# Third dense pair of a graph network kernel: half of its node batches moved beside two convolutions, raw rows looked up again

## The reference, cut to what matters

```python
x = layernorm(x + gat3(x))        # L0: three attention layers over 4 heads, with raw x as the residual
x = layernorm(x + gcn2(x))        # L1: two convolutions, relu(agg @ W1.T + b1), relu(agg @ W2.T + b2)
x = layernorm(x + gcn1(x))        # L2: one convolution
x = layernorm(x + sage2(x))       # L3: relu(concat(h, mean of neighbours) @ W + b), twice
```

## Time and profile before

| | |
|---|---|
| median of 3 runs | 5128.42 us (5124.89 to 5132.35) |
| the profiled execution | 5132.61 us, its span 5130.8 us |
| busy share of the span | PE 77%, DVE 76%, ACT 67%, POOL 55% |
| instructions | 108022 |
| DMA | 1072.25 MB, mean 209 GB/s |
| HBM | read 607.70 MB, written 466.24 MB |

### The profile page before, as it was taken

The page is one execution under the profiler, slowest core; times in us unless marked ns, Lnnn a source line. Parts: engine busy times, 40 slices in busy tenths (PEclk is TensorE's granted clock), DMA queues, the critical chain, the costliest instruction groups (busy, mean ns, idle before and its releaser), DMA issues. The chain is left out here.

```text
span 5130.8 us, 108022 instructions
## 1 busy us (share of the span) xinstructions
PE 3927.6 (77%) x23872; PEld 2892.8 (56%) x23872; DVE 3884.4 (76%) x14954; ACT 3424.7 (67%) x11259; POOL 2796.4 (55%) x2718
## 2 busy tenths in 40 slices
PE   2999999566996898774998995897767676665554
PEld 1666766344774454663555774343666666565554
DVE  4999999676998787997886998898547777444343
ACT  0899999454886676884776885787548788333332
POOL 2888888475552122651223452112767676777777
PEclk9999999787998899997999997998888888997666
DMA  2566665597996576994676995675546565543332
GB/s 62 165 187 196 202 194 190 194 331 274 355 353 220 196 242 209 328 326 152 228 241 234 349 350 189 221 225 170 157 152 202 187 208 189 156 146 113 96 97 72
DMA packets 612938, 1072.25 MB, mean 209 GB/s; under 512 B 107736, under 2 KB 128362, under 8 KB 612764
## 3 DMA queue, kind: packets, MB, share of 16 engines
q1 hardware_dynamic: 537308, 944.74, 54.2%
q0 software_dynamic: 75456, 125.65, 9.2%
HBM read 607.70 MB, written 466.24 MB: 209 GB/s over the span
## 5 line engine op out<-in xcount | busy, mean ns | idle before, releaser
L2409 POOL DMA_INDIRECT got_c<-table,src_row x980 | 931.3, 950 | 378.8 <-issue 296.5
L1410 POOL DMA_INDIRECT src_got_s<-table,src_row x588 | 554.4, 943 | 497.4 <-PE bank L1456 119.4
L1994 POOL TENSOR_TENSOR part_m<-part_m,half_sum_m 128x512 f32<-128x512 f32 x147 | 220.7, 1501 | 916.8 <-DVE half_sum_m L2210 916.8
L2437 PE MATMUL bank<-pick_c,got_c 128*128 128x128 f32 x1960 | 348.3, 333 | 407.9 <-DMA got_c<-table,src_row 337.2
L2003 PE MATMUL bank<-w_all,dt_m 128*128 128x512 f32 x1176 | 568.7, 600 | 35.4 <-DMA dt_m<-delta_t 33.6
L2437 PEld LDWEIGHTS bank<-pick_c,got_c 128*128 128x128 f32 x1960 | 299.9, 234 | 453.6 <-issue 251.6
L1565 ACT ACTIVATE z_s<-z_s,shift_s,dev_s 128x128 f32<-128x128 f32 x1176 | 483.4, 485 | 2.1 <-DVE shift_s L1684 0.9
L2540 ACT COPY agg_c<-bank 128x512 f32<-128x512 f32 x245 | 143.0, 584 | 434.7 <-DVE bank L1851 281.4
L790 PEld LDWEIGHTS bank<-w_mean,ht 128*128 128x128 f32 x2352 | 313.5, 194 | 144.0 <-issue 144.0
L2461 PE MATMUL bank<-w_c,agg_c 128*128 128x128 f32 x1960 | 389.3, 328 | 2.3 <-ACT agg_c L2540 2.2
L787 PE MATMUL bank<-bias,first_row 128*128 128x512 f32 x588 | 323.6, 632 | 38.1 <-ACT ht L850 13.8
(11 more groups left out here) (327 smaller groups left out, 11582.0 us busy)
## 6 DMA issues: line engine op xcount, KB each, us to landing
table<-rows SPq DMA_DIRECT2D x294, 256.0 KB
x_s<-table SPq DMA_DIRECT2D x294, 256.0 KB
x_c<-table SPq DMA_DIRECT2D x245, 256.0 KB
table<-mid_s SPq DMA_DIRECT2D x196, 256.0 KB
table<-z_s SPq DMA_DIRECT2D x196, 256.0 KB
table<-z_c SPq DMA_DIRECT2D x196, 256.0 KB
own_rows_s<-table SPq DMA_DIRECT2D x147, 256.0 KB
pick_t_s<-picks_t SPq DMA_DIRECT2D x147, 256.0 KB
```

Of the source, the lines that this page charges most:

```text
L1410: nc.gpsimd.indirect_dma_start(out=src_got[r][:, g, :], out_offset=None, in_=tables[l].rows, in_offset=bass.IndirectOffsetOnAxis(ap=src_ro ...
L2409: nc.gpsimd.indirect_dma_start(out=got[r][:, g, :], out_offset=None, in_=t_in.rows, in_offset=bass.IndirectOffsetOnAxis(ap=src_row[:, t:t ...
L2437: ins = nc.tensor.matmul(b_sum[r][:, k * P:(k + 1) * P], got[b.slot][:, k, :], pick[r][:, k, :], start=k == 0, stop=sage, skip_group_check ...
```

## The change

Four things:
1. `edge_scores(2)` is called with `solo=True`. It then handles only the even node batches (0, 2, ..., 96), one in each of its 49 steps instead of two, with a step order of its own (`step_solo`) on PE, ACT, DVE and SP, and other waits that pace POOL's gathers. Buffers and banks alternate by the step's parity.
2. `convolve` takes a further argument `nodes`. With it, every second step also does one node batch of the third pair: convolution 0 does the odd batches 1 to 49, convolution 3 the batches 49, 51, ..., 97 (25 each, batch 49 in both). The node work's bias copy, PSUM to SBUF copies and normalisation are ACT's, the residual and the statistics DVE's.
3. `edge_scores(1)`: `set_by_dve` is now `(0,)`, so that PE writes the bias of h = 1, and DVE's `set_bias(b, 1)` goes.
4. The table `raw_slots` goes, with its store in `first_slots`, POOL's wait for that store and the load in `attend(2)`. There POOL gathers the raw rows again from `x`: two gathers before the addition of the batch and two after it, in a fully unrolled loop.

```diff
@@ first_slots, sync
-                            b = at(1)
-                            if b:
-                                sp.wait_ge(gathered[b.slot], b.ring4(64))
-                                sp.sem_inc(sp_pace, 1)
-                                sp.dma_start(batch_rows(raw.slots, b.batch()),
-                                             x[b.slot][:, :, :].rearrange("p g d -> p (g d)")).then_inc(raw_out[b.slot], 16)
@@ first_slots, gpsimd
-                                pool.wait_ge(raw_out[r], 16 * (b // 4))
@@ edge_scores
-                set_by_dve = (0, 1)
+                set_by_dve = (0, 1) if first else (0,)
...
@@ edge_scores, sync
+                        def step_solo(at):
+                            b = at(0)
+                            if b:
+                                loads(b)
+                            b = at(5)
+                            if b:
+                                store_middle(b, 0)
+                                store_delta(b)
+                                store_score(b)
+                            b = at(6)
+                            if b:
+                                store_rows(b, 0)
@@ edge_scores, gpsimd pace
+                            elif solo:
+                                if g == 1:
+                                    pool.wait_ge(h_made, b - 2)
+                                elif g == 2:
+                                    pool.wait_ge(y_made, b - 3)
+                                else:
+                                    pool.wait_ge(turned, b - 1)
@@ edge_scores, tensor
+                        def step_solo(at):
+                            b = at(1)
+                            if b:
+                                hidden(b, 0)
+                            b = at(2)
+                            if b:
+                                turn_delta(b)
+                                product(b, 0)
+                                turn_hidden(b, 0)
+                            b = at(3)
+                            if b:
+                                score(b)
+                            b = at(0)
+                            if b:
+                                turn_rows(b, 0)
+                            b = at(1)
+                            if b:
+                                spread(b)
@@ edge_scores, scalar: step_solo is relu(b-1), deviation(b-3), delta_out(b-2), normalise(b-3), turn_out(b), score_out(b-3)
@@ edge_scores, vector
-                            b = at(0)
-                            if b:
-                                set_bias(b, 1)
...
+                        def step_solo(at):
+                            b = at(3)
+                            if b:
+                                scale(b, 0)
+                            b = at(2)
+                            if b:
+                                residual(b, 0)
+                                middle(b, 0)
+                                moments(b, 0)
+                            b = at(1)
+                            if b:
+                                set_bias(b, 0)
+                                difference(b)
@@ attend, gpsimd
+                        if last:
+                            for b in range(nb):
+                                r = b % 2
+                                if b > 3:
+                                    pool.wait_ge(z_read, b - 3)
+                                raw_rows(b, (0, 1))
+                                pool.wait_ge(m_made, 4 * b + 4)
+                                nc.gpsimd.tensor_tensor(flat(part[r]), flat(part[r]), flat(half_sum[r]), ALU.add).then_inc(parts_added, 1)
+                                raw_rows(b, (2, 3))
@@ convolve
+                def even(b):
+                    return nodes and b and b.slot % 2 == 0
@@ convolve, sync
+                        def load_nodes(b):
+                            r = b.slot // 2
+                            hold(sp, nz_read, b.ring(1, -2))
+                            sp.sem_inc(sp_pace, 1)
+                            sp.dma_start(flat(nx[r]), batch_rows(from_rows.nodes, b.batch() + offset)).then_inc(nx_in[r], 16)
...
+                            b = at(3)
+                            if even(b):
+                                load_nodes(b)
...
+                            b = at(6)
+                            if even(b):
+                                store_node_middle(b)
+                            b = at(9)
+                            if even(b):
+                                store_nodes(b)
@@ convolve, tensor
+                        def node_turn(b):
+                            r = b.slot // 2
+                            pe.wait_ge(nx_in[r], b.ring4(16))
+                            hold(pe, nmid_made, b.ring(1, -1))
+                            for g in range(GB):
+                                ins = nc.tensor.transpose(b_turn[:, g * P:(g + 1) * P], nx[r][:, g, :], ident[:, :])
+                            ins.then_inc(n_turned, 1)
...
+                        def node_steps(at):
+                            b = at(4)
+                            if even(b):
+                                node_middle(b)
+                            b = at(5)
+                            if even(b):
+                                node_product(b)
+                            b = at(3)
+                            if even(b):
+                                node_hidden(b)
...
                         def step_gcn_relu(at):
                             b = at(1)
                             if b:
                                 sum_edges(b)
+                            node_steps(at)
                             b = at(2)
                             if b:
                                 product(b)
+                            if even(b):
+                                node_turn(b)
                             b = at(1)
                             if b:
                                 add_own(b)
@@ convolve, scalar
+                        def node_middle_out(b):
+                            r = b.slot // 2
+                            act.wait_ge(nmid_turned, b.ring(1))
+                            hold(act, nmid_stored[r], b.ring4(16, -16))
+                            nc.scalar.copy(flat(nmid[r]), b_turn[:, :]).then_inc(nmid_made, 1)
+                            hold(act, nz_read, b.ring(1, -1))
+                            nc.scalar.copy(b_node[:, :], nb2[:, :]).then_inc(n_bias, 1)
...
+                        def node_steps(at):
+                            b = at(3)
+                            if even(b):
+                                node_relu(b)
+                            b = at(4)
+                            if even(b):
+                                node_middle_out(b)
+                            b = at(6)
+                            if even(b):
+                                node_deviation(b)
+                            b = at(7)
+                            if even(b):
+                                node_normalise(b)
+
                         def step_relu(at):
                             b = at(0)
                             if b and not sage:
                                 diagonals(b)
+                            node_steps(at)
                             b = at(2 if sage else 1)
                             if b:
                                 set_bias(b)
                                 sums_out(b)
+                            b = at(2)
+                            if even(b):
+                                node_turned(b)
@@ convolve, vector, step_relu
+                            b = at(6)
+                            if even(b):
+                                node_scale(b)
                             b = at(2)
                             if b:
                                 residual(b)
+                            b = at(5)
+                            if even(b):
+                                node_residual(b)
+                                node_moments(b)
@@ the calls
-        edge_scores(2, (io["L3_gnn_W1"][0:D, :], io["c_L3_gnn_b1"]), (io["L3_gnn_W2"][0:D, :], io["b_L3_gnn_b2"]), t[6], t[7], t[8])
+        edge_scores(2, (io["L3_gnn_W1"][0:D, :], io["c_L3_gnn_b1"]), (io["L3_gnn_W2"][0:D, :], io["b_L3_gnn_b2"]), t[6], t[7], t[8], True)
...
+        third = (t[6], t[7], t[8], (io["L3_gnn_W1"][0:D, :], io["c_L3_gnn_b1"]), (io["L3_gnn_W2"][0:D, :], io["b_L3_gnn_b2"]))
+        convolve(0, "gcn0", False, t[3], t[4], None, (io["L1_gnn_W1"],), io["b_L1_gnn_b1"], third + (1,))
...
+        convolve(3, "sage", False, t[6], t[7], None, (io["L3_gnn_W1"][D:, :], io["L3_gnn_W1"][0:D, :]), io["b_L3_gnn_b1"],
+                 third + (2 * (nb - (nb + 1) // 2) + 1,))
```

More of the change, by code:

```diff
@@ L1243, in edge_scores @@
                 scores = pairs("scores", (P, P))
-                x, z = ([fours(f"{n}{h}_") for h in range(2)] for n in ("x", "z"))
+                halves = range(1 if solo else 2)
```

(31 more changed lines are left out.)

222 lines of the change are left out of this document (156 added, 66 removed).

## The result

The changed kernel takes 5277.92 us (median of 4 runs), the kernel before 5130.39 beside it: ratio 1.0285, 95% interval 1.0258 to 1.0312. The profiled execution's span is 5280.9 us, 150.1 more than before. The forecast was 5325, slower.

The account below looks back on a forecast made before the run. No engine is full; stages in a row have different limits, POOL's gather issue bounding the convolutions. Terms -67 + 25 + 253 - 9 - 8 + 2 = +196 us on 5128.4 gave 5325 us, range 5215 to 5445.

Parts of the forecast that it names:

- Fourth convolution: ACT and PE take turns because node steps precede the sums; 20.1 us a pair, 512 us against 259, +253.
- 17.7 at full clock: Fourth convolution: a pair of steps from PE's 9.94, ACT's 7.33 and four hand-overs of 0.1 us, PE unthrottled.
- Rival 1: Fourth convolution: ACT's node work is hidden, costing 25 us; whole kernel 5096 us, faster; 7%.
- rival 2: Fourth convolution: PE falls to its lower clock level for most of it, 628 us; whole kernel 5441 us; 13%.
- Third score stage: Solo halves the dense batches; a loop through PE and DVE then bounds the step at 6.1 us, 326 against 393, -67.
- First convolution: Node work makes PE and ACT as long as POOL's period; 10.7 us a pair plus 8 us at the end, +25.
- late nx load: First convolution: upper bound of +68 us, 12.5 us a pair, if the nx load lands after PE wants it.
- Second score stage: Bias moves from DVE, the fullest engine, to PE, the new limit at about 6.15 us a step, -9.
- slots: Slots stage: 49 stores of 256 KB and POOL's wait for them go, -8, bounds 0 and -17.
- Last message pass: Raw load leaves SP and 196 gathers come to POOL, covered by 0.67 us a step if they stay 0.95 us, +2.
- rival 4: Last message pass: POOL's addition comes late, DVE's two-input operations lengthening gathers, +34; whole kernel 5357 us; 4%.
- the 0.17 that the slack held: Last message pass: POOL's addition is late if the gathers grow by over 0.17 us each; slack 0.67 us a step.

Follow-up runs that it names:

- h: Changed kernel plus two thrown-away 512-wide products on PE in each fourth-convolution step with node work: 5207.96 us, ratio 1.0150 to the kernel before.
- a_sums_first: Changed kernel with ACT's set_bias and sums_out ahead of its node steps in the fourth convolution; on slow gathers 5627.97 us, ratio 0.9984 to the kernel before.
- b: Changed kernel with only ACT's square root and normalising operations moved behind sums_out in the fourth convolution: 5723.40 us, ratio 1.0152 to the kernel before, slow gathers.

## Why the prediction was right, point by point

**Fourth convolution (+253, measured +256).** The mechanism and the size held. The step that carried it was to read both engines' new orders for the same n and to ask which item of ACT's step PE's product waits for. That the number came out within 3 us is in part luck, since two terms missed and cancel. A pair was put at 20.1 us and took 20.0 on average, 20.45 in the steady part. ACT's items with four hand-overs were put at 7.7 us, and PE's pauses for them are 6.6 (2.87 + 3.78 in the pair shown): the items were added by their durations, but each starts before the record of the one ahead ends (copy to copy 0.48 us, 0.59 long), and a hand-over takes 0.04 to 0.06 us, not 0.1. PE's own part was put at 12.4 and took 13.4 (13.8 in the pair shown), which is 1.35 to 1.39 times the 9.94 and not 1.25 (start and drain took 34 us, not 30): the assumed clock was a choice between ends of 1 and 1.73, and its reason, the first convolution's 0.85, was thin. The working's 17.7 at full clock carries the same excess: with 6.6 it is 16.5, and h, at 0.92, has 16.9. Rival 1 (hidden hand-over) and rival 2 (628 us) did not come. Rival 1's condition had a slip: with 21 us of start and drain 57 us more allow a pair of 12.3 us, not 11.5; at 20 neither matters. The low end of the range had one too: 57 us less in the fourth convolution and 33 less by solo lead from 5325 to 5235, not 5215.

**Third score stage (-67, measured -96): the mis-sized term.** The loop was named rightly, its length was not: 6.1 us against 5.5. I added durations. What counts is from start to start, and that is shorter, as the changed kernel's trace shows: on DVE 0.60 us from the residual to the copy, 0.69 and 0.68 long, and on PE 0.50 from the transposes to the product, where the transposes are 0.66 long:

```profile
2900.52 0.69 DVE L1716 SCALAR_TENSOR_TENSOR z_s<-bank,x_s 128x512 f32<-128x512 f32 x1 [1.04 <-PE bank L1471]
...
2901.12 0.68 DVE L1710 COPY mid_s<-bank 128x512 f32<-128x512 f32 x1
...
2904.34 0.66 PE L1492 MATMUL bank<-ident,delta_s 128*128 128x128 f32 x4 [0.78 <-DVE delta_s L1703]
...
2904.84 1.06 PE L1471 MATMUL bank<-w_s,ht_s 128*128 128x128 f32 x8
```

**First convolution (+25, measured +14).** Two steps stayed at POOL's 10.0 us; the gathers run from 3463.1 to 3707.2 as tightly as before. The 0.7 us a pair that I added for two engines that are as long as POOL was not there. The drain behind the last gather was larger than the 8 us: 3735.8 - 3708.2 = 28 us, where it was 13. The late nx load that I bounded at +68 is real and small, and POOL's lead of four batches hides it (waits view, first convolution):

```profile
POOL got_c L2531 <- issue: 58.5, 192, 0.3
...
PE bank L2599 <- DMA nx_c<-table: 23.5, 20, 2.8
```

**Second score stage (-9, measured -15)** and **slots (-8, measured -4)**: within their bounds, right in sign; for the first the reason (DVE full, PE next) is not shown, since on slow gathers undoing it gained.

**Last message pass (+2, measured -2).** Right in size by luck: the reason given, gathers of 0.95 us, was wrong. (The -2 itself is no gain: other quick traces of the same stage are up to 1.6 us longer.) I wrote that no row of gathers shows the contention of the Trainium skill's page (GPSIMD Engine Reference, Specifications). The groups view and the timeline of the changed kernel do:

```profile
L2052 POOL DMA_INDIRECT x_m<-in_x_dram,dst_node x196 | 222.5, 1135 | 100.7 <-issue 52.0 <-POOLq L117 48.4
L2062 POOL TENSOR_TENSOR part_m<-part_m,half_sum_m 128x512 f32<-128x512 f32 x49 | 62.5, 1275 | 7.2 <-DVE half_sum_m L2280 6.4
```

```profile
3300.98 1.31 POOL L2052 DMA_INDIRECT x_m<-in_x_dram,dst_node  x1 [0.30 <-issue]
3302.60 1.36 POOL L2052 DMA_INDIRECT x_m<-in_x_dram,dst_node  x1 [0.30 <-issue]
...
3305.42 0.96 POOL L2052 DMA_INDIRECT x_m<-in_x_dram,dst_node  x1 [0.16 <-issue]
```

```profile
3300.80 0.68 DVE L2304 TENSOR_TENSOR rows_m<-rows_m,x_m 128x512 f32<-128x512 f32 x1
...
3302.47 0.68 DVE L2312 SCALAR_TENSOR_TENSOR rows_m<-rows_m,x_m 128x512 f32<-128x512 f32 x1
```

The two gathers under DVE's two operations with both inputs in SBUF take 1.31 and 1.36 us, the one under others 0.96. So it is over the whole stage: 94 of the 196 gathers start while such an operation runs and share over 0.3 us with it, and they take 1.19 to 1.45 us, the other 102 at most 0.97. But it matters which starts first. Where the gathers are slow the two engines shift against each other, and then a gather can start before DVE's operation (a_sums_first, POOL and then DVE):

```profile
3390.59 0.94 POOL L2052 DMA_INDIRECT x_m<-in_x_dram,dst_node  x1 [0.30 <-issue]
```

```profile
3390.63 0.69 DVE L2304 TENSOR_TENSOR rows_m<-rows_m,x_m 128x512 f32<-128x512 f32 x1
```

The overlap is 0.69 us, and the gather still takes 0.94. Of the gathers in that run that share over 0.3 us with such an operation, the 54 that started first took 0.94 or 0.95 us and the 18 that started second 1.19 to 1.41. DVE's operation is no longer in either case. The contention of the page is there, then, but only for the gather that comes second, and it waits for no more than the rest of DVE's operation, where the prediction's +34 us (rival 4) took the whole 0.68 for each. In the changed kernel the mean is 1.135, 0.19 more than elsewhere, just beyond the 0.17 that the slack held: POOL now stands idle only 7.2 us in 49 steps before its addition (330.6 us before). It is full, and the step is still (3442.9 - 3110.5)/48 = 6.93 us. That the stage didn't grow is a matter of hundredths. My comparison of 0.95 at 88% and 49% DVE load was the wrong one, since the DVE operations there read PSUM.

## What to carry to other kernels

When work is put beside other work, write down for one step index what each engine does in order, and mark where an engine's new item waits for its partner in the same step while the partner waits for something behind that item: ACT was 68% idle before the change, and the cost was still PE's work and ACT's items ahead of the hand-over in turn, cured by moving one call behind the items that others wait for. Length of a loop through engines is counted from start to start, not by durations. And a stage that is tuned to the pace of gathers should be timed where they are slow as well, since its gain can vanish there.

## What the runs showed of the hardware that was not expected

- The pace of gathers differs between the groups of runs, with the kernel before at 5638 us on chip 15 and 5700 on chip 11, in every execution, and at 5128 on chips 4 and 10: in the unedited third convolution 263 against 329 us, POOL's instructions equally long. A difference between chips is the nearest reading, but no chip is on record at two times, so the occasion can't be told from the chip. What POOL waits for is open: the waits view gives 45.5 us in 28 waits of that stage to a DMA, but by the name of a transfer of an earlier stage, so the name can't be right; and the DMA share is lower there (0.51 against 0.62), not higher.
- The granted clock answers to PE's pauses in both directions: pauses of 2.9 and 3.8 us in a pair gave 0.75, the same records with pauses of 2.3 and 2.7 us (b) 0.86, with 1.88 us of thrown-away products in each pause (1.2 and 2.1 us of it left) 0.92, with hardly a pause 1.00. These are means of the two levels: in the pair shown the products behind the pause mostly take 0.63 us for two records, against 0.39 at a granted clock of 1.00. Adding work to PE made the kernel 70 us faster.
- A gather that starts while DVE runs a 512-wide operation with two SBUF inputs is up to 0.5 us longer (1.19 to 1.45 instead of 0.94); one that starts just ahead of such an operation is not longer at all, nor is DVE's operation.
